# The residual sum of an attention layer: from a VectorE addition to a second matmul with an identity

## The chip, the core and the metric

The kernel runs on one core of one Trainium2 chip. The metric is the device time of one execution in microseconds. A core has five engines that work side by side, each through its own list of instructions in order: TensorE (PE in the profile, with its weight loads as PEld), VectorE (DVE), ScalarE (ACT), GpSimd (POOL) and SyncE (SP), which only issues DMAs here. They meet through semaphores: an instruction may wait until a counter has reached a value, and raises another one when it is done.

## What is computed

The reference is one layer of an audio tower over 16 batches of 375 x 64 values. Each batch gives 367 rows (tokens) of 128 features.

```python
h = tok(x, kernel, bias)                    # convolution over 9 taps, scaled, tanh, relu
h = h + attn(layernorm(h), ...)             # three banded softmaxes over one score matrix
h = h + ffn(layernorm(h), ...)              # product-key expert lookup, 8 heads, top 16 of 64 x 64

def attn(x, Wq, bq, Wk, bk, Wo, bo, gamma, beta):
    q, k = x @ Wq + bq, x @ Wk + bk
    acc = sum(softmax(banded(q @ k.T / sqrt(128))) @ x for 3 band widths) / 3
    res = x + (acc @ Wo + bo)
    return layernorm(res) * gamma + beta
```

The change is in the line `res = x + (acc @ Wo + bo)`. All of this part is in float32.

## The kernel before

**Tiling.** A batch's 367 rows stand in three tiles of 124 partitions (they overlap a little), the feature axis of 128 along the free dimension. The expert lookup (the "ffn") works on the flat list of all 5872 rows in 46 tiles of 128, so three of its tiles fall to one batch.

**Staging.** Everything is written out by hand. For every engine there is a function `body(c)` that lists its steps for one turn of the loop, and the loop runs over the batches. One turn mixes work of several batches: the attention of batch c or c + 1, the convolution of c + 1 or c + 2, and the ranking and expert steps (`rank`, `choose`, `one_high`, `low_weights`, `product`, `finish`) of c - 1 and c - 2. Nothing reorders an engine's list at run time: a step whose input is late holds up all that stands behind it on its engine.

**The steps around the sum**, by engine, for a batch:

- GpSimd, `p1_xb`: xb = xl + bo, where xl is the normalised input of the attention; one instruction over 124 x 384, done early.
- TensorE, `p1_wo`, once for each of three tiles t: axT (the attention's result, transposed) times `wo_sb`, into columns (1 + t) * 128 of `bankC`, a bank of PSUM. It stands on TensorE between the steps `p1_ax`, `p1_turn_attn`, `scatter` and `q_product`. After the third, `wo_done` stands at 3 for this batch.
- VectorE, `p1_res`: waits for all three, then res = bankC + xb over 124 x 384, into SBUF.
- VectorE, `p1_stats(c, 1)` and `p1_moments(c, 1)`: mean and variance of each row of res (bn_stats into `bns`, bn_aggr into `bna`).
- GpSimd, `p1_rstd(c, 1)`: `lnr` = (variance + eps) ** -0.5, in two instructions.
- VectorE, `p1_shift(c, 1)`: `lnm` = -mean * lnr. ScalarE, `p1_ln(c, 1)`: xh = res * lnr + lnm, three instructions.
- GpSimd, `p1_h`: three instructions over 124 x 384 that make `hsum` (xh * gamma + beta + h0).
- VectorE, `p1_stats(c, 2)`: bn_stats of `hsum`, the first step of the next layer norm.

On GpSimd these steps stand in a list with work of the expert lookup. From GpSimd's `body`, a little shortened (c is there one turn behind):

```python
each(q_scale, c, 1)          # waits for VectorE's nmx
each(rank_sums, c, 0, 2)
each(select, c, 0)
each(normalise, c, 0)        # its first instruction waits for VectorE's wrec
do(p1_rstd, c + 1, 1)
each(q_std, c, 2)
do(p1_h, c + 1)
each(rank_sums, c, 1, 0)
```

The names in the rows below: `nmx` is VectorE's result of `q_guard`, which `qscale` on GpSimd takes; `wrec` the reciprocals of `invert_sums`; `wn` and `wcell` the results of `normalise`; `std`, `qvar` and `qguard` those of `q_std`; `val`, `idx` and `scores` those of `rank`; `banks` is the group of banks that bankC belongs to.

Of the kernel before, what the change touches and what calls it, by code (L numbers as in the profile page):

```python
# [8 lines left out]
TAPS, D = 9, 128  # L9
T = L - TAPS + 1  # L10
NT = 124
# [59 lines left out]
def build(nc, x, tok_kernel, tok_bias, wq, bq, wk, bk, wo, bo, gamma, beta, fwq, fbq, lng, lnb,  # L71
# [5 lines left out]
    with ctx:  # L77
        def sb(name, shape, dt=f32):
            return ctx.enter_context(nc.sbuf_tensor(name, shape, dt))

        def sem(name):
            return ctx.enter_context(nc.semaphore(name))
# [12 lines left out]
        id32 = sb("id32", [128, 128])  # L95
# [11 lines left out]
        wq_sb, wk_sb, wo_sb = sb("wq_sb", [D, D]), sb("wk_sb", [D, D]), sb("wo_sb", [D, D])  # L107
# [54 lines left out]
        xb = sb("xb", [NT, 3, D])  # L162
# [8 lines left out]
        diag = sb("diag", [NT, 3, NT])  # L171
        attnT = sb("attnT", [NT, 3 * NT])
        axT = sb("axT", [D, NT])
        res = sb("res", [NT, 3, D])
        xh = sb("xh", [NT, 3, D])
        h = [sb(f"hsum{p}", [NT, 3, D]) for p in range(2)]
        hn = sb("hn", [NT, 3, D])
# [53 lines left out]
        bankA, bankB, bankC = (banks3[:, i * 512:(i + 1) * 512] for i in range(3))  # L231
        bankQ = ctx.enter_context(nc.psum_tensor("bankQ", [128, 512], f32))
        bankS = ctx.enter_context(nc.psum_tensor("bankS", [128, 1024], f32))
        bankM = ctx.enter_context(nc.psum_tensor("bankM", [128, 1024], f32))
        wcT_ps = bankS[0:2 * NC, :].bitcast(f16).rearrange("p (k n) -> p k n", k=2)
        merged = bankM[:, :].rearrange("p (k n) -> p k n", k=2)
        coef = bankM[:, 0:NG * EL * TG].rearrange("p (g l t) -> p g l t", g=NG, l=EL)
# [32 lines left out]
        xb_ready = sem("xb_ready")  # L270
# [8 lines left out]
        ax_done = sem("ax_done")  # L279
        axT_ready = sem("axT_ready")  # L280
        wo_done = sem("wo_done")
        res_ready = sem("res_ready")
        xh_ready = sem("xh_ready")
        h_ready = sem("h_ready")
        hn_ready = sem("hn_ready")
# [57 lines left out]
        def wait(eng, s, value):  # L343

            if not isinstance(value, int) or value > 0:
                eng.wait_ge(s, value)
# [45 lines left out]
        def do(step, c, *rest):  # L392

            if c.exists:
                step(c, *rest)

        def each(step, c, t, *rest):

            if c.has(t):
                step(c, t, *rest)  # L400
# [135 lines left out]
        def _(pool):  # L536
# [93 lines left out]
            def p1_xb(c):  # L630
                b = c.b
                pool.wait_ge(xl_ready, b + 1)
                wait(pool, res_ready, b)
                g.tensor_tensor(xb[:, :, :], xl[:, :, :], bob.unsqueeze(1).to_broadcast([NT, 3, D]), ALU.add).then_inc(xb_ready, 1)

            def p1_h(c):
# [85 lines left out]
            def body(c):  # L722
# [30 lines left out]
                each(rank_sums, c, 2, 2)  # L753
                do(p1_sbias, c + 2, 0)
                do(p1_xb, c + 2)
                each(q_scale, c + 1, 0)
                do(p1_sbias, c + 2, 1)
# [322 lines left out]
        def _(pe):  # L1080
            e = nc.tensor
# [122 lines left out]
            def p1_wo(c, t):  # L1204
                b, n = c.b, c.tile(t)
                pe.wait_ge(axT_ready, n + 1)
                e.matmul(bankC[0:NT, (1 + t) * D:(2 + t) * D], axT[:, :], wo_sb[:, :], start=True, stop=True).then_inc(wo_done, 1)

            def p1_turn_hn(c):
                b = c.b  # L1210
# [101 lines left out]
            def body(c):  # L1312
# [7 lines left out]
                each(merge_cells, c + -2, 2)  # L1320
                each(q_score, c + -1, 1)
                do(p1_wo, c, 0)
                do(p1_ax, c, 1)
                do(p1_turn_attn, c, 2)
                do(p1_wo, c, 1)
                do(p1_ax, c, 2)
                each(scatter, c + -2, 2)
                do(p1_wo, c, 2)
                each(q_product, c + -1, 2)
                each(experts_out, c + -2, 2)  # L1330
# [42 lines left out]
        def _(dve):  # L1373
            v = nc.vector
# [86 lines left out]
            def p1_stats(c, i):  # L1461

                b = c.b
                src = (h0, res, h[c.par])[i]
                if i == 0:
                    dve.wait_ge(h0_ready, 2 * (b + 1))
                elif i == 1:
                    dve.wait_ge(res_ready, b + 1)
                else:
                    dve.wait_ge(h_ready, 3 * (b + 1))  # L1470
                for t in range(3):
                    last = v.bn_stats(out=bns[i][:, t, :], in_=src[:, t, :])
                last.then_inc(ln_stats[i], 1)
# [32 lines left out]
            def p1_rden(c, t):  # L1506
# [1 line left out]
                dve.wait_ge(probs_ready, n + 1)  # L1508
                wait(dve, diag_ready, n)
                v.reciprocal(rden[:, :], den[:, :]).then_inc(rden_ready, 1)  # L1510

            def p1_res(c):
                b = c.b
                dve.wait_ge(wo_done, 3 * (b + 1))
                dve.wait_ge(xb_ready, b + 1)
                wait(dve, xh_ready, b)
                v.tensor_tensor(res[:, :, :].rearrange("p t d -> p (t d)"), bankC[0:NT, D:4 * D],
                                xb[:, :, :].rearrange("p t d -> p (t d)"), ALU.add).then_inc(res_ready, 1)

            def q_guard(c, t):  # L1520

# [113 lines left out]
            def body(c):  # L1635
# [6 lines left out]
                each(rank, c + -1, 1, 0, 0)  # L1642
                each(rank, c + -1, 1, 0, 1)
                each(invert_sums, c + -1, 0)
                do(p1_res, c)
                each(product, c + -2, 2)
                do(p1_stats, c, 1)
                do(p1_moments, c, 1)
                each(rank, c + -1, 1, 0, 2)
# [4 lines left out]
                each(rank, c + -1, 1, 1, 1)  # L1654
                each(rank, c + -1, 1, 1, 2)
                do(p1_stats, c, 2)
                do(p1_moments, c, 2)
                each(rank, c + -1, 1, 1, 3)
# [11 lines left out]
                each(choose, c + -1, 1, 1)  # L1670
                each(choose, c + -1, 1, 2)
                do(p1_stats, c + 1, 0)
                each(rank, c + -1, 2, 0, 0)
                do(p1_moments, c + 1, 0)
# [61 lines left out]


            run(dve, start, body, lambda: None)


# [20 lines left out]
```

## Time and profile before

| | |
|---|---|
| time, median of 3 runs | 1364.64 us (1363.95 to 1365.32) |
| profiled execution: time / span | 1364.77 us / 1363.0 us |
| VectorE busy | 1241.4 us, 91% of the span |
| TensorE busy (matmuls) | 1012.5 us, 74% |
| GpSimd busy | 925.8 us, 68% |
| ScalarE busy | 901.4 us, 66% |
| TensorE's granted clock, mean | 0.761 of full speed |
| bytes moved by DMA | 16.56 MB, 12 GB/s |

The span is what lies between the first and the last instruction; the execution's own time has 1.8 us more around it. Busy is the time in which an engine executes; an engine that waits for a semaphore is idle. A share of the whole span is a mean over the start (some 340 us, in which the loop fills), 12 turns of about 80 us that look alike, and the end.

### The profile page before, as it was taken

The page shows a single profiled execution, that of the slowest core. Times are in us where ns is not written, and L with a number is a line of the kernel's source. Part 1 is how long each engine was busy: PE and PEld are TensorE (multiplying, and loading weights), DVE is VectorE, ACT ScalarE, POOL GpSimd, SP SyncE. Part 2 cuts the span into 40 slices and gives each one's busy share as a digit, 9 for nine tenths or more (in the row PEclk, how much of TensorE's full clock was granted, in tenths as well). Part 3 has the DMA queues.
Part 4 walks back from the last instruction along what each step waited for, and adds up shares of the span by engine and source line. Part 5 has one row for each costly group of instructions (what it writes and reads, how often), then busy time and mean ns, then how long its engine had stood idle before and what let it go on. Part 6 is the DMA issues. An engine that isn't in the chain of part 4 may idle for free.

```text
span 1363.0 us, 38569 instructions
## 1 busy us (share of the span) xinstructions
PE 1012.5 (74%) x9443; PEld 659.5 (48%) x9443; DVE 1241.4 (91%) x9666; ACT 901.4 (66%) x4045; POOL 925.8 (68%) x1881
## 2 busy tenths in 40 slices
PE   2746777877878877887888788788867878877644
PEld 1514454645445554644555464455635545453433
DVE  4529696999999999999999999999999999999994
ACT  1546857577686867768686776868577686857442
POOL 4336666685868768586876858677685867768561
PEclk8867777679787786878777787877688787776665
DMA  2010000000000000000000000000000000000000
GB/s 56 7 28 3 9 13 10 11 13 11 14 3 23 4 13 13 12 13 4 23 5 13 13 12 13 4 23 4 13 13 11 13 4 17 4 8 13 6 6 7
DMA packets 35682, 16.56 MB, mean 12 GB/s; under 512 B 15392, under 2 KB 35248, under 8 KB 35458
## 3 DMA queue, kind: packets, MB, share of 16 engines
q1 hardware_dynamic: 34834, 13.81, 4.2%
q8 instruction: 75, 1.23, 0.4%
q14 instruction: 149, 1.22, 0.3%
q10 hardware_dynamic: 624, 0.30, 0.1%
HBM read 7.58 MB, written 6.01 MB: 10 GB/s over the span
## 4 chain that ended last, share of the span: by engine, by line
DVE 49%; ACT 13%; PE 12%; POOL 12%; issue 10%; SPq 1%; DMA 1%; DVEq 0%; POOLq 0%; ACTq 0%
DVE idx L1549 12%; DVE val L1547 7%; DVE scores L1552 6%; DVE oh L1562 6%; DVE cr L1620 6%; PE banks L1135 3%; DVE best L1618 3%; DVE wl L1582 3%; ACT ns_junk L942 3%; DVE masked L1502 2%; ACT act_g L919 2%; ACT eh L997 2%; POOL ce L691 2%; POOL std L654 2%; PE bankQ L1236 2%
## 5 line engine op out<-in xcount | busy, mean ns | idle before, releaser
L1549 DVE FIND_INDEX8 idx<-val,scores 128x8 uint16<-128x64 f32 x1472 | 298.0, 242 | 0.1
L1547 DVE MAX8 val<-scores 128x8 f32<-128x64 f32 x1472 | 205.6, 230 | 0.2
L1300 PE MATMUL bankM<-wl,oh 128*128 128x16 f16 x5888 | 161.0, 172 | 56.4 <-DVE wl L1582 52.4
L665 POOL TENSOR_TENSOR qscale<-nmx,power 128x16 f32<-128x16 f32 x46 | 151.1, 3284 | 60.9 <-DVE nmx L1526 60.9
L1300 PEld LDWEIGHTS bankM<-wl,oh 128*128 128x128 f16 x5888 | 157.1, 101 | 71.6 <-DVE wl L1582 61.6
L1552 DVE MATCH_REPLACE8 scores<-val,scores 128x64 f32<-128x64 f32 x736 | 149.6, 233 | 0.0
L1562 DVE TENSOR_SCALAR oh<-eh 128x1024 f16<-128x1024 int16 x368 | 134.1, 429 | 12.6 <-ACT eh L997 12.3
L1549 DVE MATCH_VALUE_LOAD idx<-val,scores 128x8 f32 x1472 | 140.2, 95 | 0.0
L942 ACT ACTIVATE ns_junk<-bankQ 128x32 f32<-128x32 f32 x736 | 132.8, 269 | 5.2 <-PE bankQ L1253 5.1
L942 ACT ACTIVATION_READ_ACCUMULATOR ns_junk<-bankQ 128x1 f32 x736 | 133.1, 282 | 0.0
L979 ACT ACTIVATE wcell<-wn 128x400 f16<-128x400 f32 x46 | 24.9, 542 | 136.6 <-POOL wn L716 136.6
L691 POOL TENSOR_TENSOR cs<-val_s 128x64 f32<-128x64 f32 (+4 forms) x460 | 110.1, 274 | 7.2
L1263 PE MATMUL bankS<-wgk,hnT 128*128 128x512 f32 x184 | 112.7, 698 | 0.0
L1188 PE MATMUL banks<-diag,probs 124*124 124x124 f32 x672 | 100.7, 313 | 15.3 <-ACT diag L876 15.2
L1188 PEld LDWEIGHTS banks<-diag,probs 124*124 124x124 f32 x672 | 98.5, 227 | 24.2 <-ACT diag L876 18.6
L685 POOL TENSOR_TENSOR val_s<-val,qscale 128x128 f32<-128x128 f32 x92 | 43.7, 475 | 80.6 <-DVE val L1547 80.5
L1308 PE MATMUL bankM<-up_x,prod 128*128 128x128 f32 x368 | 77.9, 379 | 26.2 <-DVE prod L1591 26.2
L1222 PE MATMUL bankQ<-hnT,down_x 128*128 128x384 f32 (+1 forms) x128 | 70.8, 642 | 32.9 <-ACT act_g L919 18.6
L1274 PE MATMUL bankS<-id,wcell 128*100 128x128 f16 x552 | 52.4, 262 | 48.7 <-POOL wcell L719 47.6
L1308 PEld LDWEIGHTS bankM<-up_x,prod 128*128 128x128 f32 x368 | 70.2, 284 | 35.8 <-DVE prod L1591 35.3
L928 ACT ACTIVATE sq_junk<-bankQ 128x64 f32<-128x64 f32 x368 | 75.7, 235 | 10.3 <-PE bankQ L1237 10.3
L997 ACT ACTIVATE eh<-bankM,digit_bias 128x256 int16<-128x256 f32 x184 | 73.4, 507 | 9.1 <-PE bankM L1285 9.1
(199 smaller groups left out, 3033.5 us busy)
## 6 DMA issues: line engine op xcount, KB each, us to landing
h_in<-h_rows SPq DMA_DIRECT2D x45, 64.0 KB, 2.7
out<-o_sb SPq DMA_DIRECT2D x45, 64.0 KB, 1.5
x_in<-in_x SPq DMA_DIRECT2D x16, 93.8 KB
x_in<-in_x SPq DMA_DIRECT2D x16, 62.5 KB
h_rows<-hsum SPq DMA_DIRECT2D x16, 62.0 KB
h_rows<-hsum SPq DMA_DIRECT2D x16, 61.0 KB
h_rows<-hsum SPq DMA_DIRECT2D x16, 60.5 KB
x_in<-in_x SPq DMA_DIRECT2D x16, 31.0 KB
```

Source lines behind the costliest of these rows:

```text
L665: g.tensor_tensor(qscale[c.slot(t)][:, :, :].rearrange("p h s -> p (h s)"), nmx[:, :, :].rearrange("p h s -> p (h s)"), power[0:QT, 0, :], ...
L691: g.tensor_tensor(dst[:, :, at:at + m], src[:, :, 0, a:a + 1].to_broadcast([QT, k, m]), src[:, :, 1, 0:m], ALU.add)
L942: last = a.activation(ns_junk[:, i, :], bankQ[0:QT, i * HALF:(i + 1) * HALF], ACT.Square, accum_out=nss[:, i // 2, i % 2:i % 2 + 1])
L997: last = a.activation(eh[:, j, :, :], merged[:, :, 2 * QT:3 * QT], ACT.Identity, bias=digit_bias[:, j:j + 1], scale=1.0 / EL)
L1188: last = e.matmul(bankB[0:NT, k * NT:(k + 1) * NT], probs[t][w][:, OFF[k]:OFF[k] + NT], diag[:, w, :], start=w == windows[0], stop=w == wi ...
L1263: e.matmul(part, hnT[c.par][:, QT * t:QT * (t + 1)], wgk[:, 2 * k:2 * k + 2, :].rearrange("p k n -> p (k n)"), start=True, stop=False)
L1300: last = e.matmul(coef[:, g, :, :], oh[:, k, g, :, :].rearrange("p v t -> p (v t)"), wl[:, part, k, :, TG * g:TG * (g + 1)], start=k + par ...
L1308: last = e.matmul(ffn, prod[:, l, :], up_x[:, l, :], start=l == 0, stop=l == EL - 1)
L1547: last = v.max(out=v_[:, hd, s, best8], in_=src[:, hd, s, :])
L1549: last = v.max_index(out=i_[:, hd, s, best8], in_max=v_[:, hd, s, best8], in_values=src[:, hd, s, :])
L1552: last = v.match_replace(out=src[:, hd, s, :], in_to_replace=v_[:, hd, s, best8], in_values=src[:, hd, s, :], imm_value=NEG)
L1562: last = v.tensor_scalar(by_shift[:, :, :, value, :], eh[:, :, :, :].rearrange("p s k (g t) -> p s (k g) t", t=TG), float(value), None, AL ...
```

## The change

`p1_res` is gone from VectorE. In its place `p1_wo` issues a second matmul for each tile: the identity matrix `id32` times `xb`, accumulated onto the projection in the same PSUM columns (`start=False`). `res` is now a name for those PSUM columns, so that `p1_stats(c, 1)` on VectorE and `p1_ln(c, 1)` on ScalarE read PSUM where they read SBUF. TensorE waits once per batch for `xb`; those who waited for `res_ready` wait for `wo_done`.

```diff
-        res = sb("res", [NT, 3, D])
+        res = bankC[0:NT, D:4 * D].rearrange("p (t d) -> p t d", d=D)
...
             def p1_xb(c):
                 b = c.b
                 pool.wait_ge(xl_ready, b + 1)
-                wait(pool, res_ready, b)
+                wait(pool, wo_done, 3 * b)
...
             def p1_wo(c, t):
                 b, n = c.b, c.tile(t)
                 pe.wait_ge(axT_ready, n + 1)
-                e.matmul(bankC[0:NT, (1 + t) * D:(2 + t) * D], axT[:, :], wo_sb[:, :], start=True, stop=True).then_inc(wo_done, 1)
+                if t == 0:
+                    pe.wait_ge(xb_ready, c.b + 1)
+                out_t = bankC[0:NT, (1 + t) * D:(2 + t) * D]
+                e.matmul(out_t, axT[:, :], wo_sb[:, :], start=True, stop=False)
+                e.matmul(out_t, id32[0:NT, 0:NT], xb[:, t, :], start=False, stop=True).then_inc(wo_done, 1)
...
                 elif i == 1:
-                    dve.wait_ge(res_ready, b + 1)
+                    dve.wait_ge(wo_done, 3 * (b + 1))
...
-            def p1_res(c):
-                b = c.b
-                dve.wait_ge(wo_done, 3 * (b + 1))
-                dve.wait_ge(xb_ready, b + 1)
-                wait(dve, xh_ready, b)
-                v.tensor_tensor(res[:, :, :].rearrange("p t d -> p (t d)"), bankC[0:NT, D:4 * D],
-                                xb[:, :, :].rearrange("p t d -> p (t d)"), ALU.add).then_inc(res_ready, 1)
...
                 each(invert_sums, c + -1, 0)
-                do(p1_res, c)
                 each(product, c + -2, 2)
                 do(p1_stats, c, 1)
```

VectorE's list in a turn in the middle of the program, from the reciprocals `wrec` on, before and then after:

```order
L1632 RECIPROCAL wrec<-wsum 128x8 [waits chosen,weights]
L1517 TENSOR_TENSOR res<-banks,xb 124x384 [waits xh_ready,xb_ready,wo_done]
L1591 TENSOR_TENSOR prod<-bankM,act_g 128x32x4x4 [waits ffn_done,gelu_done,scattered]
L1472 BN_STATS bns<-res 124x6 [waits res_ready]
L1472 BN_STATS bns<-res 124x6 x2
L1482 BN_AGGR bna<-bns 124x2 [waits ln_stats1,ln_rstd1]
```

```order
L1627 RECIPROCAL wrec<-wsum 128x8 [waits chosen,weights]
L1586 TENSOR_TENSOR prod<-bankM,act_g 128x32x4x4 [waits ffn_done,gelu_done,scattered]
L1475 BN_STATS bns<-banks 124x6 [waits wo_done]
L1475 BN_STATS bns<-banks 124x6 x2
L1485 BN_AGGR bna<-bns 124x2 [waits ln_stats1,ln_rstd1]
```

The sum has left the list, and the statistics now wait for TensorE themselves; the order of all else is as it was.

TensorE's list of the same turn, from the first `p1_wo` to `q_product` (`diag`, `probs` are the softmax, `wl`, `oh` the scatter of the expert lookup), before and then after:

```order
L1207 MATMUL banks<-wo_sb,axT 124x128 [waits axT_ready]
L1200 MATMUL banks<-attnT,xl 128x124 [waits axT_ready,attnT_ready]
L1200 MATMUL banks<-attnT,xl 128x124 x2
L1188 MATMUL banks<-diag,probs 124x124 [waits attnT_ready,diag_ready]
L1188 MATMUL banks<-diag,probs 124x124 x5
L1207 MATMUL banks<-wo_sb,axT 124x128 [waits axT_ready]
L1200 MATMUL banks<-attnT,xl 128x124 [waits axT_ready,attnT_ready]
L1200 MATMUL banks<-attnT,xl 128x124
L1300 MATMUL bankM<-wl,oh 128x16 [waits high_ready,onehigh_ready,wm_ready,wl_ready]
L1300 MATMUL bankM<-wl,oh 128x16 x127
L1207 MATMUL banks<-wo_sb,axT 124x128 [waits axT_ready]
L1236 MATMUL bankQ<-fwqT,hnT 128x512 [waits nss_ready,carried,hnT_ready]
```

```order
L1209 MATMUL banks<-wo_sb,axT 124x128 [waits xb_ready,axT_ready]
L1210 MATMUL banks<-xb,id 124x128
...
L1209 MATMUL banks<-wo_sb,axT 124x128 [waits axT_ready]
L1210 MATMUL banks<-xb,id 124x128
L1199 MATMUL banks<-attnT,xl 128x124 [waits axT_ready,attnT_ready]
L1199 MATMUL banks<-attnT,xl 128x124
L1303 MATMUL bankM<-wl,oh 128x16 [waits high_ready,onehigh_ready,wm_ready,wl_ready]
L1303 MATMUL bankM<-wl,oh 128x16 x127
L1209 MATMUL banks<-wo_sb,axT 124x128 [waits axT_ready]
L1210 MATMUL banks<-xb,id 124x128
L1239 MATMUL bankQ<-fwqT,hnT 128x512 [waits nss_ready,carried,hnT_ready]
```

Each of the three has a companion behind it, two of them ahead of the scatter and one between the scatter and `q_product`.

## Rows read from the trace of the kernel before

**Rows 1.** Page, part 1; then windows of 80 us, columns as named.

```profile
PE 1012.5 (74%) x9443; PEld 659.5 (48%) x9443; DVE 1241.4 (91%) x9666; ACT 901.4 (66%) x4045; POOL 925.8 (68%) x1881
...
580.00:660.00 80.00, 62.65 (x625) 40.35 (x621) 79.31 (x630) 57.09 (x260) 59.61 (x122) 0.80 0.04 12
```

**Rows 2.** VectorE's waits, 340 to 1230 us: total us, times, longest us.

```profile
DVE bna L1482 <- DVE bns L1472: 4.3, 23, 0.5
DVE lnm L1489 <- POOL lnr L622: 1.1, 4, 0.3
DVE oh L1562 <- ACT eh L997: 1.0, 3, 0.4
```

**Rows 3.** VectorE in order of time around the sum: start, duration, instruction.

```profile
582.64 0.53 DVE L1517 TENSOR_TENSOR res<-banks,xb 124x384 f32<-124x384 f32 x1
583.06 0.70 DVE L1591 TENSOR_TENSOR prod<-bankM,act_g 128x512 f32<-128x512 f32 x1
583.66 0.69 DVE L1472 BATCH_NORM_STATS2 bns<-res 124x6 f32<-124x128 f32 x3
```

**Rows 4.** GpSimd in order of time, same turn.

```profile
575.76 3.90 POOL L665 TENSOR_TENSOR qscale<-nmx,power 128x16 f32<-128x16 f32 x1 [4.14 <-DVE nmx L1526]
...
583.45 0.86 POOL L716 TENSOR_TENSOR wn<-wsel,wrec 128x400 f32<-128x400 f32 x1
...
586.12 0.86 POOL L622 TENSOR_TENSOR lnr<-lnv,power 124x3 f32<-124x3 f32 x1
...
591.72 1.00 POOL L644 TENSOR_TENSOR hsum<-hsum,h 124x384 f32<-124x384 f32 x1
```

**Rows 5.** VectorE in order of time, same turn, at nmx, lnm and the next statistics.

```profile
575.51 0.17 DVE L1526 TENSOR_TENSOR nmx<-nss,qguard 128x16 f32<-128x16 f32 x1
...
587.48 0.15 DVE L1489 SCALAR_TENSOR_TENSOR lnm<-bna,lnr 124x3 f32<-124x3 f32 x1
...
591.65 1.13 DVE L1547 MAX8 val<-scores 128x8 f32<-128x64 f32 x8
592.75 0.68 DVE L1472 BATCH_NORM_STATS2 bns<-hsum 124x6 f32<-124x128 f32 x3
```

**Rows 6.** The same place, first and last of the 12 turns: GpSimd, VectorE.

```profile
352.96 1.00 POOL L644 TENSOR_TENSOR hsum<-hsum,h 124x384 f32<-124x384 f32 x1
353.99 0.29 DVE L1472 BATCH_NORM_STATS2 bns<-hsum 124x6 f32<-124x128 f32 x1
...
1228.75 1.00 POOL L644 TENSOR_TENSOR hsum<-hsum,h 124x384 f32<-124x384 f32 x1
1229.78 0.68 DVE L1472 BATCH_NORM_STATS2 bns<-hsum 124x6 f32<-124x128 f32 x3
```

**Rows 7.** First batch: VectorE and GpSimd in order of time.

```profile
54.95 0.56 DVE L1517 TENSOR_TENSOR res<-banks,xb 124x384 f32<-124x384 f32 x1 [0.98 <-DVE key_z L1434]
55.54 0.68 DVE L1472 BATCH_NORM_STATS2 bns<-res 124x6 f32<-124x128 f32 x3
...
61.62 0.99 POOL L644 TENSOR_TENSOR hsum<-hsum,h 124x384 f32<-124x384 f32 x1
...
62.65 0.68 DVE L1472 BATCH_NORM_STATS2 bns<-hsum 124x6 f32<-124x128 f32 x3 [4.56 <-POOL hsum L644]
```

**Rows 8.** TensorE in order of time, near 580 and near 980 us.

```profile
580.23 0.77 PE L1207 MATMUL banks<-wo_sb,axT 128*124 128x128 f32 x2
580.79 1.91 PE L1236 MATMUL bankQ<-fwqT,hnT 128*128 128x512 f32 x2
582.63 0.39 PE L1237 MATMUL bankQ<-fbq,ones 3*128 3x512 bf16 x1
...
982.59 0.60 PE L1237 MATMUL bankQ<-fbq,ones 3*128 3x512 bf16 x1
```

**Rows 9.** ScalarE, first of `q_squares` near 580; VectorE, the sum near 980.

```profile
584.78 0.21 ACT L928 ACTIVATE sq_junk<-bankQ 128x64 f32<-128x64 f32 x1
...
981.44 0.54 DVE L1517 TENSOR_TENSOR res<-banks,xb 124x384 f32<-124x384 f32 x1
```

More of the change, by code:

```diff
@@ L281, in build @@
         wo_done = sem("wo_done")
-        res_ready = sem("res_ready")
         xh_ready = sem("xh_ready")
```

## The prediction

> **What bounds the kernel now.** I read the page's busy shares first. VectorE is the busiest engine with 91% of the span, and in the windows of 80 us it is at 79.31 us of 80, where TensorE has 62.65, ScalarE 57.09 and GpSimd 59.61 [rows 1]. The list of VectorE's waits over the 890 us from 340 to 1230 us confirms it: single waits of at most 0.5 us, 6.4 us in all, most of it between bn_stats and bn_aggr, which is VectorE waiting for itself [rows 2]. By this view every instruction that VectorE loses should shorten the kernel.
>
> The next view says otherwise, and it is the one on which this prediction stands: the time order of VectorE and GpSimd side by side, in the turn around 580 us. GpSimd waits 4.14 us for VectorE's `nmx`, which starts at 575.51, and begins `qscale` at 575.76 [rows 4, 5]. From there to the end of the third `hsum` instruction at 591.72 + 1.00 = 592.72 it works through its list. None of the rows behind `qscale` shows a wait for VectorE [rows 4]. VectorE has 17.24 us of its own work in the same stretch, from 575.51 to the statistics of `hsum` at 592.75 [rows 5]. So two paths leave `nmx` and meet at `bns<-hsum`, and they end within a few hundredths of a microsecond. Which one is the later?
>
> The waits that are plain give the measure. In the first batch VectorE stood idle 4.56 us for `hsum`; that ended at 61.62 + 0.99 = 62.61 and the statistics began at 62.65, 0.04 later [rows 7]. In the turn at 580 us the distance is 592.75 - 592.72 = 0.03. In the first of the 12 like turns it is 353.99 - 353.96 = 0.03 and in the last 1229.78 - 1229.75 = 0.03 [rows 6]; in 11 of the 12 it is 0.02 to 0.04, and in one (at 911 us) it is 0.09. The other side agrees: on VectorE an instruction that need not wait begins some 0.10 us before its predecessor's recorded end (583.06 against 582.64 + 0.53, and 583.66 against 583.06 + 0.70 [rows 3]), but `bns<-hsum` begins only 0.03 before the end of MAX8 (591.65 + 1.13 = 592.78 [rows 5]). VectorE is held there by some 0.07 us already. The wait is hidden in the idle column, because recorded durations overlap. At this place GpSimd's list is the bound, or level with VectorE's.
>
> **The change part by part.**
>
> *The sum leaves VectorE.* It takes 0.53 us, but its successor starts 583.06 - 582.64 = 0.42 us after it [rows 3], so 0.42 us per batch come free, 16 x 0.42 = 6.7 us in all. They come free between `nmx` and `bns<-hsum`. Does GpSimd's path get shorter with it? Its releasers are `nmx` and `wrec`, both ahead of the sum on VectorE; `wn` runs at 583.45, well behind `wrec`. The one input behind the sum is `bna` for `lnr`, and ScalarE's `xh` for `hsum`. `lnr` runs at 586.12, 1.5 us behind the stretch of the statistics that starts at 583.66 and lasts 0.69, in GpSimd's own order. So GpSimd ends at 592.72 as before, and VectorE's 0.42 us turn into a wait ahead of `bns<-hsum`. What is late next is nothing: VectorE goes on from the same moment. Gain in each of these turns: 0.42 minus 0.42, that is 0; in the turn at 911 us, where VectorE is the later one by some 0.06, that much. I take 0.1 us for all of them.
>
> On the way it passes `lnm`, which needs `lnr`: that ends at 586.12 + 0.86 = 586.98 and `lnm` starts at 587.48 [rows 4, 5]. With 0.42 less `lnm` would start at 587.06, still 0.08 behind, so that no wait is needed there. If one comes, it is a part of the same 0.42.
>
> *The first batch.* Here all is one chain, and the statistics start 55.54 - 54.95 = 0.59 after the sum [rows 7]. The sum leaves the chain and the third identity product enters it. A projection's step on TensorE takes 580.79 - 580.23 = 0.56 in the slow stretch [rows 8]; between half of that and all of it makes the gain 0.0 to 0.3. I take 0.2. In the next three batches the statistics of `hsum` are not at the tie everywhere, but `lnm` ahead of them already waits 0.3 us for GpSimd's `lnr`, which is the same block one step earlier: nothing to gain.
>
> *TensorE gets three products per batch.* Each is like the `wo` product in size, 0.28 to 0.56 us, so 0.8 to 1.7 us per batch, 13 to 27 us in all on an engine that has 17 us free in each 80 [rows 1]. What stands behind them: ahead of the scatter nothing on VectorE waits for long, and behind it `q_product`, whose result ScalarE takes in `q_squares`. That one starts at 584.78 [rows 9], while `q_product` ends at 582.63 + 0.39 = 583.02 [rows 8]: 1.76 us of cover, enough even for all three products at the slow step. The turn near 980 us is the exception: there `q_product` ends at 982.59 + 0.60 = 983.19 [rows 8], and the sum of that turn starts at 981.44 [rows 9], so `q_squares` would start at 983.58 by the distance of the other turn (584.78 - 582.64 = 2.14). The cover is 0.4 us, and up to 1.3 us stick out, which go through `qvar` into `hsum` and so into VectorE's wait. Between 0 and 1.3 I take 0.3 us, since GpSimd's place for `qvar` absorbs some of it. Without cover in every turn this would cost at worst 1.3 us each time; that is a rival below.
>
> *Statistics and xh from PSUM.* No row shows bn_stats from PSUM. The sum itself reads 384 values per partition from PSUM in 0.53 us, three statistics of 128 from SBUF take 0.69 [rows 3]. I take no difference, and at most 0.1 us for each, 0.3 per batch. It would be paid from the 0.42 us of spare time, so it costs nothing. The same holds for the new wait of the statistics on TensorE: they would start near 583.2, and `wo` of the third tile ends at 580.23 + 0.77 = 581.00 with 0.56 to come.
>
> *The buffers.* `xb` and `axT` are held a little differently, and `xb` stands ready long before TensorE wants it. Cost 0.
>
> The sum against the profiled execution: 1364.77 - 0.1 - 0.2 + 0.3 = 1364.8. The median is 0.13 us below that execution, so 1364.6 us.
>
> **The rivals.** A measurement of this kernel can tell about 0.2% from no change, 2.7 us.
>
> *A. VectorE is the bound, and its time comes back in full.* For it: 99% busy in the loop [rows 1]. Against it: the 0.03 us of rows 4 to 7. It would give 1364.6 - 6.7 = 1357.9 us, or 1362.7 if the statistics cost 0.3 more per batch (16 x 0.12 = 1.9). It decides if GpSimd's part gets shorter as VectorE's does. The page Perfetto Trace Analysis of the Trainium skill, section Identifying the Most-Contended Engine, says to take the engine of highest occupancy and optimise that first; by that rule this rival would be the forecast, and the trace agrees only as far as the busy shares go. The skill's page VectorE: DVE Perf Modes, section on the TRN2 errata, gives an instruction that reads PSUM 62 cycles more than one that reads SBUF; as an estimate that is 0.19 us per batch for three statistics, which would leave rival A 3.7 us. Chance 0.09.
>
> *B. TensorE comes late for `q_squares`, not in one turn but in most.* For it: the turn near 980 us shows that TensorE's work can slide that far. Against it: 1.76 us of cover in the common turn. It decides where the added products exceed the cover. At 0.5 us in 12 turns it gives 1364.6 + 6 = 1370.6 us, at 0.3 us 1368.2. Chance 0.05.
>
> *C. Part of the gain goes through.* Turns rearrange a little: a turn in which VectorE is later by 0.1 to 0.3 us keeps that much. At 0.2 us in 15 turns 1361.6 us. For it: the turn at 911 us. Chance 0.07, half of it beyond 2.7 us.
>
> *No change, as forecast*: chance 0.79, by itself within 1363.4 to 1366.0.
>
> **How the numbers follow.** Faster by over 0.2%: rival A and a half of C, 0.12. Slower by over 0.2%: B and a little for what I don't see, 0.06. Within 0.2%: the rest, 0.82. The range holds the forecast's own and C's upper part: 1361.8 to 1366.2.
>
> **What would show it.** In the trace after, VectorE's wait list has `bns<-hsum` for GpSimd's `hsum` in nearly every turn, 0.3 to 0.4 us each, some 5 us in all, where now there is none in that stretch; the distance from `hsum`'s end to the statistics stays 0.03 to 0.04; the distance from `nmx` to `bns<-hsum` stays 17.24; a turn stays 79.6 us. VectorE's busy time falls by some 7 us at the same span. TensorE's rises by 13 to 27. I would be wrong if `nmx` to `bns<-hsum` fell to 16.9 (GpSimd's list got shorter), or if `hsum` ended later than 17.2 us behind `nmx` (TensorE or ScalarE holds GpSimd up).

## The result and the profile after

Measured in turn with the kernel before, the changed kernel takes 1362.14 us (median of 17 runs, 1359.40 to 1363.85), the kernel before 1364.84 us (17 runs, 1363.71 to 1365.32). The ratio is 0.9981, 95% interval 0.9974 to 0.9988: 2.7 us less, 0.19%, just inside what counted as no change. The forecast was 1364.6 us with a range of 1361.8 to 1366.2. One thing stands out before any trace is opened: the changed kernel's runs spread over 4.4 us, those of before over 1.6.

The page after, part 1 (as [rows 1]): busy time and share of the 1360.4 us span.

```profile
PE 1022.2 (75%) x9539; PEld 668.3 (49%) x9539; DVE 1233.1 (91%) x9650; ACT 900.3 (66%) x4045; POOL 922.5 (68%) x1881
```

VectorE lost 1241.4 - 1233.1 = 8.3 us of work, TensorE gained 1022.2 - 1012.5 = 9.7. VectorE's waits over the same stretch as in [rows 2]: total us, times, longest us.

```profile
DVE bna L1485 <- DVE bns L1475: 4.2, 24, 0.2
DVE bns L1475 <- POOL hsum L643: 4.1, 11, 0.4
DVE lnm L1492 <- POOL lnr L621: 0.9, 3, 0.3
DVE oh L1557 <- ACT eh L996: 0.7, 2, 0.4
```

The second row is new, and it is the wait that was forecast: 11 times, 0.37 us each. The same turn as in [rows 3 to 5], VectorE in order of time with GpSimd's last `hsum` instruction from its own list:

```profile
574.39 0.17 DVE L1521 TENSOR_TENSOR nmx<-nss,qguard 128x16 f32<-128x16 f32 x1
...
581.55 0.64 DVE L1586 TENSOR_TENSOR prod<-bankM,act_g 128x512 f32<-128x512 f32 x1
582.10 0.69 DVE L1475 BATCH_NORM_STATS2 bns<-banks 124x6 f32<-124x128 f32 x3
...
590.58 0.99 POOL L643 TENSOR_TENSOR hsum<-hsum,h 124x384 f32<-124x384 f32 x1
...
590.27 0.97 DVE L1542 MAX8 val<-scores 128x8 f32<-128x64 f32 x7
591.61 0.49 DVE L1475 BATCH_NORM_STATS2 bns<-hsum 124x6 f32<-124x128 f32 x2 [0.37 <-POOL hsum L643]
```

From `nmx` to `prod` VectorE needs 581.55 - 574.39 = 7.16 us; before it was 583.06 - 575.51 = 7.55 [rows 3, 5]. From `nmx` to the statistics of `hsum` it is 591.61 - 574.39 = 17.22 us; before 17.24. GpSimd's `hsum` ends at 590.58 + 0.99 = 591.57, and the statistics start 0.04 later. So what VectorE saves ahead of `prod` it gives back in front of `bns<-hsum`: at all 12 places in the loop the statistics start 0.03 to 0.04 us behind the end of `hsum`. On this path nothing is left of the gain.

Yet the turns became shorter elsewhere. The first and last of the 12 statistics of `hsum`, as in [rows 6]:

```profile
353.74 0.68 DVE L1475 BATCH_NORM_STATS2 bns<-hsum 124x6 f32<-124x128 f32 x3 [0.37 <-POOL hsum L643]
...
1226.53 0.68 DVE L1475 BATCH_NORM_STATS2 bns<-hsum 124x6 f32<-124x128 f32 x3 [0.37 <-POOL hsum L643]
```

That is 872.79 us for 11 turns, 79.34 each; before it was 1229.78 - 353.99 = 875.79, 79.62 each [rows 6]. The 3.0 us are not spread evenly. Before, one turn of 11 was under 79.3 us, after it are five (79.28, 79.05, 79.04, 79.04, 79.08). Most turns are some 79.55 or some 79.05 us long, with few in between. That looks like a switch, and not like a saving in every turn.

**What the switch is.** TensorE before, in the turn near 425 us, in order of time. `L1274` is `turn_cells`, twelve small products that need GpSimd's `wcell`, and `L1135` the convolution of a later batch.

```profile
423.53 0.60 PE L1237 MATMUL bankQ<-fbq,ones 3*128 3x512 bf16 x1
424.63 2.07 PE L1308 MATMUL bankM<-up_x,prod 128*128 128x128 f32 x8 [0.50 <-DVE prod L1591]
426.77 1.52 PE L1274 MATMUL bankS<-id,wcell 128*100 128x128 f16 x12
428.08 4.00 PE L1135 MATMUL banks<-xT,conv_w 128*128 128x367 f32 x10
```

The same place after the change:

```profile
421.38 0.63 PE L1210 MATMUL banks<-xb,id 124*124 124x128 f32 x2
...
423.65 0.60 PE L1240 MATMUL bankQ<-fbq,ones 3*128 3x512 bf16 x1
424.19 1.94 PE L1311 MATMUL bankM<-up_x,prod 128*128 128x128 f32 x8
426.50 0.87 PE L1277 MATMUL bankS<-id,wcell 128*100 128x128 f16 x12 [0.37 <-POOL wcell L718]
427.20 3.50 PE L1134 MATMUL banks<-xT,conv_w 128*128 128x367 f32 x10
```

Before, TensorE stood 0.50 us for VectorE's `prod` and then ran `experts_out` (`bankM<-up_x,prod`) and `turn_cells` slowly: 1.52 us for twelve products that take 0.87 after. The convolution took 4.00 us, after it 3.50. The granted clock of these stretches says why. Windows, TensorE alone: length, busy time (instructions), granted clock (PEclk), DMA share, GB/s. Before:

```profile
424.63:426.77 2.14, 2.07 (x9) 0.50 0.00 0
426.77:428.08 1.31, 1.31 (x12) 0.50 0.02 6
```

and after:

```profile
424.19:426.40 2.21, 1.94 (x9) 0.62 0.00 0
426.40:427.20 0.80, 0.70 (x12) 1.00 0.04 10
```

Before, the clock stands at its lower level, 1.2 GHz, through both, and its mean over the convolution is 0.87; after, it rises to 2.4 GHz during `experts_out`, so that `turn_cells` and the convolution run at full clock (1.00). The convolution then ends at 430.70 instead of 432.08. Counted from the turn's statistics of `hsum` (433.28 after, 433.57 before), it ends 2.58 us ahead of them instead of 1.49.

**How that reaches VectorE.** The steps behind the convolution can be followed on ScalarE. Before, in order of time:

```profile
432.30 0.27 ACT L935 ACTIVATE std96T<-bankQ 96x128 bf16<-96x128 f32 x1 [1.15 <-PE bankQ L1243]
...
443.29 0.22 ACT L928 ACTIVATE sq_junk<-bankQ 128x64 f32<-128x64 f32 x1 [0.46 <-PE bankQ L1237]
...
464.58 1.59 ACT L997 ACTIVATE eh<-bankM,digit_bias 128x256 int16<-128x256 f32 x4
```

ScalarE after:

```profile
430.92 0.27 ACT L934 ACTIVATE std96T<-bankQ 96x128 bf16<-96x128 f32 x1 [0.57 <-PE bankQ L1246]
...
442.25 0.22 ACT L927 ACTIVATE sq_junk<-bankQ 128x64 f32<-128x64 f32 x1
...
463.47 1.56 ACT L996 ACTIVATE eh<-bankM,digit_bias 128x256 int16<-128x256 f32 x4
```

`std96T` comes 1.38 us earlier, the first of `q_squares` 1.04, the `eh` shown 1.11. VectorE takes that `eh` in `oh`. VectorE before, in order of time:

```profile
465.08 0.99 DVE L1618 MAX8 best<-cr 128x8 f32<-128x50 f32 x8
466.20 1.63 DVE L1562 TENSOR_SCALAR oh<-eh 128x1024 f16<-128x1024 int16 x4
467.75 0.21 DVE L1569 TENSOR_SCALAR el<-expert 128x256 int16<-128x256 int16 x1
```

The first of the four `oh` instructions by itself, before and then after:

```profile
466.20 0.60 DVE L1562 TENSOR_SCALAR oh<-eh 128x1024 f16<-128x1024 int16 x1
...
465.96 0.41 DVE L1557 TENSOR_SCALAR oh<-eh 128x1024 f16<-128x1024 int16 x1
```

And VectorE's list after, in order of time; it comes to this place at the same moment:

```profile
465.06 0.98 DVE L1613 MAX8 best<-cr 128x8 f32<-128x50 f32 x8
465.96 1.41 DVE L1557 TENSOR_SCALAR oh<-eh 128x1024 f16<-128x1024 int16 x4
467.30 0.22 DVE L1564 TENSOR_SCALAR el<-expert 128x256 int16<-128x256 int16 x1
```

From MAX8 to `el` it is 2.67 us before and 2.24 after: 0.43 us. Half of it stands ahead of `oh` (466.20 is 0.13 behind MAX8's recorded end, 465.96 is 0.08 ahead of it). There VectorE was waiting in the kernel before: `oh` needs all four pieces of `eh`, the last ends at 464.58 + 1.59 = 466.17, and `oh` starts 0.03 later, the same distance as at `hsum`. After the change `eh` ends at 465.03, 0.93 ahead of `oh`. The other half is the first `oh` instruction, which takes 0.60 us instead of 0.41; the program has no wait inside the four, and why this one is longer isn't shown. So in this turn the late convolution costs VectorE some 0.4 us half a turn later, and the change spares it that. The steps from one instruction to the next are not clean: this turn keeps 0.17 us of the 0.43 (79.45 before, 79.28 after), since some 0.2 us went elsewhere in VectorE's ranking, in a pause to which the trace gives no releaser. The lengths of whole turns are the better measure.

It isn't the same place in every turn. In five of the 11 turns before, this `oh` starts 0.03 us behind `eh`. In the four turns whose convolution ends last, it starts 0.44 to 0.46 us behind, and VectorE has lost time earlier in the turn: they are the four in which it waits for `lnr` ahead of `lnm`, 0.15 to 0.3 us each [rows 2].

### The profile page after: what moved, and what is told of

The parts are those of the page before. It is cut to its first block, busy times and chain, and to the rows that moved or that the text cites. A ratio compares the mean times of both kernels' runs of the same rounds, so it can differ in the third digit from the quotient of the medians.

```text
span 1360.4 us, 38746 instructions
## 1 busy us (share of the span) xinstructions
PE 1022.2 (75%) x9539; PEld 668.3 (49%) x9539; DVE 1233.1 (91%) x9650; ACT 900.3 (66%) x4045; POOL 922.5 (68%) x1881
## 4 chain that ended last, share of the span: by engine, by line
DVE 53%; POOL 16%; issue 10%; ACT 10%; PE 9%; SPq 1%; DMA 1%; DVEq 0%; POOLq 0%; ACTq 0%
DVE idx L1544 12%; DVE val L1542 7%; DVE cr L1615 7%; DVE oh L1557 6%; DVE scores L1547 6%; DVE best L1613 4%; DVE wl L1577 3%; DVE masked L1505 2%; POOL std L653 2%; PE banks L1134 2%; ACT ns_junk L941 2%; POOL ce L690 2%; POOL wsel L708 1%; POOL wcell L706 1%; POOL wn L715 1%
## 5 line engine op out<-in xcount | busy, mean ns | idle before, releaser
L1544 DVE FIND_INDEX8 idx<-val,scores 128x8 uint16<-128x64 f32 x1472 | 292.3, 218 | 0.0
L1542 DVE MAX8 val<-scores 128x8 f32<-128x64 f32 x1472 | 202.2, 209 | 0.7 <-issue 0.6
L1547 DVE MATCH_REPLACE8 scores<-val,scores 128x64 f32<-128x64 f32 x736 | 145.5, 209 | 0.0
L1544 DVE MATCH_VALUE_LOAD idx<-val,scores 128x8 f32 x1472 | 105.9, 72 | 0.1
L627 POOL TENSOR_TENSOR sbias<-smax,minus_scale 124x3 f32<-124x3 f32 x48 | 9.3, 194 | 104.0 <-DVE smax L1505 104.0
```

What stands on the lines that cost most here:

```text
L1542: last = v.max(out=v_[:, hd, s, best8], in_=src[:, hd, s, :])
L1544: last = v.max_index(out=i_[:, hd, s, best8], in_max=v_[:, hd, s, best8], in_values=src[:, hd, s, :])
L1547: last = v.match_replace(out=src[:, hd, s, :], in_to_replace=v_[:, hd, s, best8], in_values=src[:, hd, s, :], imm_value=NEG)
```

## The experiments

The experiments ran on three chips, and the ratios are to the kernel before on the same chip: it took 1364.10 us on that of e1 to e4, 1364.79 on that of e5 to e8, 1364.61 on that of e9 to e11. "Short turns" counts those of 11 that took at most 79.3 us, in one trace of each kernel. That trace isn't always of a typical run: e2's is the fastest of its 12 (1362.23 us), e7's the slowest of its nine (1362.56). Against what was expected, e4 and e6 came out faster than any range given, by 2.9 and 1.7 us, and e10 0.5 us below the nearer of its two; e2, e3 and e5 fell 0.03 to 0.14 us beside the range they speak for.

### The parts alone: e1, e2, e3

**e1** is the kernel before with the products added and nothing taken off. They are overwritten by the projection behind them, so the result is that of before.

```diff
+                if t == 0:
+                    pe.wait_ge(xb_ready, c.b + 1)
+                e.matmul(out_t, id32[0:NT, 0:NT], xb[:, t, :], start=True, stop=True)
                 e.matmul(out_t, axT[:, :], wo_sb[:, :], start=True, stop=True).then_inc(wo_done, 1)
```

> The kernel before, its sum on VectorE kept, with the three identity products added on TensorE ahead of each projection and overwritten by it. Theory 1 (the 0.42 us saved on VectorE is lost at the wait for hsum, and the 2.7 us measured come from TensorE's added work, after which its clock is full in more of the convolutions): as fast as the change, 1361 to 1363 us, and more turns of 79.05 to 79.3 us than the one of before. Theory 2 (part of VectorE's saved time gets through): not faster than before, 1364 to 1366 us, since only work is added.

Measured: 1364.26 us, ratio 0.9999 (0.9990 to 1.0008), no short turn, mean turn 79.61 us. Added work alone doesn't move the time, either way.

**e2** is the changed kernel without the products; it leaves the attention's input out of the sum.

```diff
-                e.matmul(out_t, axT[:, :], wo_sb[:, :], start=True, stop=False)
-                e.matmul(out_t, id32[0:NT, 0:NT], xb[:, t, :], start=False, stop=True).then_inc(wo_done, 1)
+                e.matmul(out_t, axT[:, :], wo_sb[:, :], start=True, stop=True).then_inc(wo_done, 1)
```

> The changed kernel without its identity products, so that the attention's input is left out of the sum: VectorE's sum is gone and TensorE has no more work than before. Theory 1: close to before, 1364 to 1365 us, with a wait of about 0.37 us for hsum in each turn. Theory 2: as fast as the change or faster, 1361 to 1362.5 us.

Measured: 1363.86 us, ratio 1.0003 (0.9994 to 1.0011), two short turns in the trace of its fastest run; its runs spread from 1362.23 to 1368.17 us. VectorE loses its sum here too, and waits for `hsum` as in the changed kernel:

```profile
DVE bns L1471 <- POOL hsum L643: 3.7, 10, 0.4
```

So VectorE's freed time is worth nothing by itself: that part of the prediction stands.

**e3** is the changed kernel with VectorE's old instruction back in its place, into a tile that nobody reads.

```diff
                 each(invert_sums, c + -1, 0)
+                do(copy_res, c)
                 each(product, c + -2, 2)
```

> The changed kernel with VectorE's old instruction put back at its place, its result read by nobody: 0.42 us more on VectorE per batch, all else as changed. Theory 1: as the change, 1361 to 1363.5 us, with the wait for hsum gone. Theory 2: back to before, 1364 to 1366 us.

Measured: 1363.97 us, ratio 0.9999 (0.9990 to 1.0008), no short turn; the wait for `hsum` is gone from VectorE's list. Each theory that gave the 2.7 us to one part fell here: products without the shorter list give 0 (e1, e3), the shorter list without products gives 0 (e2). The effect needs both. What both act on is the start of `experts_out`: the products fill TensorE ahead of it, and `prod` releases it 0.42 us sooner. With both, the 0.50 us of idle time shown above disappears, and TensorE comes 0.33 us later than `prod` ends (near 425 us: 424.19 against 423.86).

### The meeting point: e4, e5

**e4** is the changed kernel with one round of `rank`, which stood behind the statistics of `hsum`, cut in two, and the first half put ahead of them. VectorE then has work while GpSimd finishes `hsum`.

```diff
+                each(rank, c + -1, 1, 1, 3, (0,))
                 do(p1_stats, c, 2)
                 do(p1_moments, c, 2)
-                each(rank, c + -1, 1, 1, 3)
+                each(rank, c + -1, 1, 1, 3, (1,))
```

> The changed kernel with half of a rank step (four value loads and four index searches, 0.77 us) moved ahead of the statistics of hsum on VectorE, so that VectorE has work while GpSimd finishes hsum. If the wait of 0.37 us in 12 turns is what the saved time turned into, it goes and the turn gets shorter by about as much: 1362.1 - 4.4 = 1357.7 us, 1357 to 1359.5. If something else holds the turn at its length, the wait turns up elsewhere and the time stays at 1361 to 1363 us.

Measured: 1354.11 us, ratio 0.9927 (0.9915 to 0.9940), 10.0 us less than the kernel before on its chip, and 8.0 less than the change, measured on another. GpSimd and VectorE in order of time, in the turn around 580 us:

```profile
588.45 1.00 POOL L643 TENSOR_TENSOR hsum<-hsum,h 124x384 f32<-124x384 f32 x1
...
589.66 0.23 DVE L1544 FIND_INDEX8 idx<-val,scores 128x8 uint16<-128x64 f32 x1
589.79 0.67 DVE L1475 BATCH_NORM_STATS2 bns<-hsum 124x6 f32<-124x128 f32 x3
```

`hsum` ends at 589.45 and the statistics start at 589.79, 0.34 behind it instead of 0.04, with no wait. That confirms that GpSimd's list held VectorE there. It gave more than the 4.1 us of the wait, and more than its expectation allowed for: the mean turn is 78.66 us and in 10 of 11 turns `turn_cells` and the convolution run at full clock (0.87 and 3.50 us), so that nearly every turn has both the 0.4 us of VectorE's sum and the 0.5 us of the clock.

**e5** makes the same split in the kernel before.

> The kernel before with the same half rank step moved ahead of the statistics of hsum. If the 0.37 us wait is born of the change, there is little to relieve here: the hidden 0.07 us in 12 turns, so 1363 to 1364.5 us, and the split version of the changed kernel (1354.1) stays ahead by the sum's 0.42 us in 12 to 15 turns, 5 to 6.5 us, and more. Rival: the move is worth 8 to 10 us by itself, whatever the sum, then about 1355 us.

Measured: 1364.63 us, ratio 1.0001 (0.9992 to 1.0010), no short turn. With the half round ahead of them the statistics start 0.76 to 0.94 us behind `hsum`, so there VectorE's own list ends last and the split has nothing to give. The 0.07 us per turn by which the prediction says VectorE is held already would be 0.8 us; 0.2 us were seen, and the interval is too wide to tell.

### TensorE's gap: e6, e7, e8

**e6** changes nothing on VectorE: two products of 128 x 128 are put ahead of TensorE's wait for `prod`, into a part of PSUM that `experts_out` then overwrites. They compute nothing.

```diff
             def experts_out(c, t):
                 m = c.flat(t)
+                if t == 2:
+                    for _ in range(2):
+                        e.matmul(ffn, id32[:, :], up_x[:, 0, :], start=True, stop=True)
                 pe.wait_ge(prod_ready, m + 1)
```

> The kernel before with two products more on TensorE in the place where it waits for prod ahead of the expert's output (their result is overwritten). If the clock rises in the convolution because TensorE has no gap there (theory 3), 1361 to 1363 us with turns of 79.05 to 79.3 us. If the gap is not what matters, 1363.5 to 1365 us.

Measured: 1359.28 us, ratio 0.9963 (0.9949 to 0.9976), 8 short turns, mean turn 79.19 us. A kernel with more work and the same results is 5.5 us faster. TensorE in one of the short turns, near 663 us:

```profile
660.22 1.22 PE L1308 MATMUL bankM<-up_x,id 128*128 128x128 f32 x4
661.24 1.58 PE L1311 MATMUL bankM<-up_x,prod 128*128 128x128 f32 x8
662.94 0.87 PE L1274 MATMUL bankS<-id,wcell 128*100 128x128 f16 x12
663.65 3.50 PE L1135 MATMUL banks<-xT,conv_w 128*128 128x367 f32 x10
```

There is no idle time ahead of `experts_out`, and `turn_cells` and the convolution run at full clock, as they do in 10 of the 11 turns. The eleventh is the one near 425 us: no idle time there either, yet `turn_cells` takes 1.52 us, the convolution 3.64, and the turn 79.82.

**e7** is the changed kernel once more, on this chip.

> The changed kernel once more, beside these. If its 2.7 us are its own, 1361.5 to 1362.7 us; if they came from the chip or the hour, 1363.5 to 1364.5 us.

Measured: 1361.50 us, ratio 0.9974 (0.9964 to 0.9984), 5 short turns in its trace. The gain of the change repeats on a second chip, by a hair over the bound.

**e8** is e3 with the old instruction one step later, behind `prod`.

```diff
                 each(product, c + -2, 2)
+                do(copy_res, c)
                 do(p1_stats, c, 1)
```

> The changed kernel with VectorE's old instruction put back, but behind prod and not ahead of it: VectorE's list is as long as before, while prod, and with it TensorE's next step, comes 0.42 us earlier. Theory 3 (what counts is TensorE's earlier start together with its added products): as the change, 1361 to 1363 us. If VectorE's length or ScalarE's earlier xh counts: 1363.5 to 1364.5 us, as with the instruction ahead of prod.

Measured: 1361.23 us, ratio 0.9973 (0.9963 to 0.9983), 7 short turns. VectorE has all its old work here and the kernel is as fast as the change. e3 and e8 differ only in which of two VectorE instructions comes first. So it isn't the removed work that pays: it is that `prod` comes 0.42 us sooner, together with the added products (without them, in e2, the earlier `prod` gives nothing). TensorE in e8, near 425 us:

```profile
423.75 1.41 PE L1314 MATMUL bankM<-up_x,prod 128*128 128x128 f32 x8
426.00 0.87 PE L1280 MATMUL bankS<-id,wcell 128*100 128x128 f16 x12 [0.84 <-POOL wcell L721]
426.71 3.50 PE L1137 MATMUL banks<-xT,conv_w 128*128 128x367 f32 x10
```

`experts_out` takes 1.41 us where the kernel before needs 2.07, and waits for nothing.

### Both at once: e9, e10, e11

e9 is the changed kernel with the split and one filler product (e6's edit, `range(1)`), e10 the kernel before with the split and two, e11 the changed kernel with one filler and no split.

> The changed kernel with the split rank step, and one overwritten product ahead of the expert's output on TensorE. The split version alone (1354.1) shows TensorE's full clock in nearly every convolution already, so little is left: 1353 to 1354.5 us.

> The kernel before with the split rank step and two overwritten products ahead of the expert's output: VectorE's sum kept, but neither the wait for hsum nor the slow clock in the way. If these two are all that stood between the change and its 0.42 us per batch, this one is slower than the split version of the changed kernel (1354.1) by 0.42 us in 12 to 15 turns: 1359 to 1360.5 us. If the sum's removal is worth nothing even then, 1354 to 1355.5 us.

> The changed kernel with one overwritten product ahead of the expert's output, rank step not split. The wait for hsum stays at 0.37 us in each turn, and the clock is full in more convolutions: 1358.5 to 1360 us, the same as the kernel before with its gap filled (1359.3), since the sum's 0.42 us are worth nothing here. If they are worth something, 1354 to 1356 us.

| | kernel before | changed kernel |
|---|---|---|
| as it is | 1364.79 (1 short turn) | 1361.50 (5) |
| filler | 1359.28 (8) | 1359.17 (9) |
| split | 1364.63 (0) | 1354.11 (10) |
| split and filler | 1358.48 (9) | 1353.97 (10) |

Times in us, from three chips whose kernel before lies within 0.7 us; the filler is two products in the kernel before and one in the changed kernel; ratios to the kernel before on the same chip: e9 0.9919 (0.9905 to 0.9932), e10 0.9956 (0.9943 to 0.9970), e11 0.9962 (0.9948 to 0.9975). The table takes the change apart. With the gap filled in both kernels the change is worth 0.1 us, which is the prediction's own case: VectorE's freed time turns into its wait. With the gap filled and the meeting point relieved it is worth 4.5 us (1358.48 to 1353.97). That is two thirds of the 16 x 0.42 = 6.7 us that leave VectorE. The two fillers differ by one product, which no run separates. The best kernels are e4 and e9, which can't be told apart: once the split is in the changed kernel, the filler has nothing left to do.

## Why the prediction held, and where it was wrong

**"Two paths leave `nmx` and meet at `bns<-hsum`", VectorE's 0.42 us turn into a wait.** Right, and shown: the wait is 0.37 us in 11 turns, 4.1 us in all (some 5 forecast), the distance from `nmx` 17.22 us (17.24), the lag behind `hsum` 0.04 (0.03 to 0.04). VectorE's busy time fell by 8.3 us where some 7 were forecast, since the sum's recorded 0.53 us count there and not its step of 0.42. e2 has the same wait at the same total time, e11 against e6 gives the change 0.1 us, and e4 frees the wait. Rival A, the full gain, is refuted: its rule, to shorten the busiest engine, would have given 6.7 us.

**"What is late next is nothing", "a turn stays 79.6".** This is the step that failed. A turn became 79.34 us on average, because 5 of 11 dropped by some 0.5 us. Two consequences of an earlier point in VectorE's list were not followed: `prod` is released 0.42 us sooner, and TensorE waits for `prod` with its longest stretch behind it. The prediction asked of TensorE's rows only how late its results might be, never how fast it would be running. The rows that would have told are in the trace of before: 0.50 us of idle time for `prod`, and behind it `turn_cells` in 1.52 us, where the other two rounds of `turn_cells` in the same turn take 0.87. Over the 11 turns this round takes 1.38 to 1.52 us, but for one: 1.07 us near 985, and that is the one short turn (79.01 us).

**TensorE's added time.** "13 to 27 us" was right for the products and wrong as the rise of TensorE's busy time, which is 9.7 us. The products' own records cover 22.7 us, shown by form in the lines after:

```profile
L1209 PE MATMUL banks<-wo_sb,axT 128*124 128x128 f32 x96 | 25.6, 356 | 5.9 <-ACT axT L890 5.9
L1210 PE MATMUL banks<-xb,id 124*124 124x128 f32 x96 | 22.7, 326 | 0.0
```

There are 96 halves, 6 per batch, 326 ns recorded for each. Near 421 us the step of a whole product is 421.81 - 421.38 = 0.43 us, inside the forecast's 0.28 to 0.56. The busy time rose by less because the records of neighbouring products overlap and because `turn_cells` and the convolution became shorter at the higher clock; how the 13 us divide between the two wasn't worked out. That TensorE would come late for `q_squares` (rival B, and the 0.3 us of the turn near 980) did not cost anything: the cover is 1.0 to 1.5 us in 11 of the 12 turns, where it was 1.4 to 2.0 in all but one, and in the turn near 902 us it is 0.04. There `q_squares` starts 0.08 us late, and the distance from `nmx` to the statistics is still 17.22.

**The first batch.** Forecast 0.2 us, measured some 0.5. The statistics of `hsum` start at 62.40, before at 62.65 [rows 7], and the run itself began 0.23 us later, by a DMA ahead of the first convolution. Two terms were mis-sized. From the start of the third `wo` product to the statistics of `res` it is 0.81 us, before 1.17: 0.36 us are gained there, above the forecast's 0.0 to 0.3, so the third product lengthens the chain by 0.23 us and not by 0.28 to 0.56. The other 0.1 us is `xh`, which ScalarE reads from PSUM in 454 ns where it took 483 from SBUF, three times in a row; the prediction had set that to no difference. The Trainium skill, page VectorE: DVE Perf Modes, section on the TRN2 errata, gives ScalarE 52 cycles less from PSUM than from SBUF; the rows agree in sign.

**The sum.** Forecast 1364.6, measured 1362.1. Between the two profiled spans lie 1363.0 - 1360.4 = 2.6 us: 3.0 from the 11 turns and 0.25 up to the first of the 12 statistics of `hsum`, less 0.65 that the end of the run is longer, from the last statistics shown to the end (133.22 us before, 133.87 after). What made the end longer wasn't looked into. Rival C had this size (1361.6 us) and another reason: it expected GpSimd's path and VectorE's to swap places in some turns. In the trace every turn has the wait or starts within 0.04 us of `hsum`, so it isn't that. That the measured time lies inside the range, 0.3 us above its lower end, is owed to the room left for rival C, and so in part to luck.

**What stays open.** Why the clock rises in one turn and not in the next is not settled. The link itself holds over all 13 traces, 143 turns: where this round of `turn_cells` took 0.87 us or less, 63 of 70 turns were short; where it took longer, 3 of 73 (79.01 in the kernel before, 79.22 and 79.26 in e2). In the kernel before, e1, e2, e3 and e5 no turn has it that short, in the changed kernel seven of 11 and in e7 five. Two of the seven are long in spite of it (79.38 and 79.54 us); in the second VectorE waits 0.39 us for a later `eh`. Filling TensorE ahead of `experts_out` is not all of it: it had no idle time there in 65 of the 70, but also in 11 of the 73. e1 has almost none in five of its turns, and its clock stays down. TensorE in e1, near 425 us:

```profile
424.57 0.60 PE L1241 MATMUL bankQ<-fbq,ones 3*128 3x512 bf16 x1
425.19 2.08 PE L1312 MATMUL bankM<-up_x,prod 128*128 128x128 f32 x8
427.32 1.47 PE L1278 MATMUL bankS<-id,wcell 128*100 128x128 f16 x12
428.63 3.50 PE L1135 MATMUL banks<-xT,conv_w 128*128 128x367 f32 x10
```

Its convolution does run at full clock, but behind a slow `turn_cells`. It ends 2.00 us ahead of the turn's statistics of `hsum`, between the 1.49 of the kernel before and the 2.58 of the changed one, and the turn is long (79.65 us). So both a slow convolution and a slow `turn_cells` ahead of it make the end late. Which activity decides the moment of the rise wasn't tried out further. It could also explain the spread, if of the changed kernel's 17 runs some have more short turns than others. That isn't shown: only two runs have a trace, with 5 short turns each and a mean of 79.34 and 79.47 us. The Trainium skill, page TensorE: Matmul & The Clock Gate, section on the HAM clock gate, says that the number of slow matmuls at the start of one and the same kernel differs from run to run; the spread of 4.4 us would fit with that, but no run here shows it.

## What to carry to other kernels

An engine that is busy 99% of the time can still be level with another engine's list: before taking work off it, measure at each place where the two meet how long after the other's end it starts (here 0.03 us), and relieve that place first, since the same 0.42 us per turn was worth 0.1 us without the split and 4.5 us with it (TensorE's gap filled in both). A short wait of TensorE ahead of a long stretch can cost more than its own length when the clock is at its lower level behind it: here 0.50 us of wait went with a convolution that ended 1.09 us later in its turn. Read the granted clock of the stretch, and try a reordering or an idle product there before anything larger. An edit can be tested by its parts and still pay only as a whole, so put the parts back one at a time from both ends.

## What the runs showed of the hardware

- Two products per turn that nobody reads made the kernel 5.5 us (0.4%) faster (e6). In the changed kernel, one made it 2.3 us faster across two chips (e11 against e7), to the same time.
- The same twelve small products took 1.52 us at a granted clock of 0.50 (1.2 GHz) and 0.87 at 1.00 (2.4 GHz); the eight products of `experts_out` took 2.07 us at 0.50, 1.16 at 1.00 (near 345 us before), and 1.94 or 1.41 where the clock rose in between.
- Reading PSUM instead of SBUF did not cost VectorE anything here. The statistics took 284 ns on average from PSUM, where they took 297 from SBUF; those of `hsum`, from SBUF in both kernels, took 288 and then 282, so that the 13 ns are no sure gain. ScalarE's `xh` took 454 where it took 483. Groups by form, after: busy us, mean ns | idle before them:

```profile
L1475 DVE BATCH_NORM_STATS2 bns<-banks 124x6 f32<-124x128 f32 x48 | 10.9, 284 | 1.2 <-PE banks L1210 1.2
L839 ACT ACTIVATE xh<-banks,lnm,lnr 124x128 f32<-124x128 f32 x48 | 18.5, 454 | 15.6 <-DVE lnm L1492 15.6
```

The Trainium skill, page VectorE: DVE Perf Modes, section on the TRN2 errata, gives VectorE 62 cycles more from PSUM; this instruction does not show them, and the row decides.
- Recorded durations on VectorE overlap by some 0.1 us per instruction, so that a wait of that size has no place in the idle column. In the kernel before `oh` starts 0.03 us behind the end of its `eh` at nine places in the 11 turns, and the list of waits has three of them [rows 2].
